# A fused transformer kernel: the last attention output ahead of the gate's exponents, half 1's logits ahead of half 0's score rows, and the eighth expert's second layer in PSUM bank 0

## The chip, the cores and the metric

The program runs on one core of one Trainium2 chip. The metric is the device time of one execution in microseconds (us), the median of three runs. The profile is one further execution of the same program, recorded by the hardware profiler.

## The reference, cut to what matters

The input x has 2 sequences of 512 tokens of width 128, and the context has 2 times 154 rows. Four blocks are added to x in turn, each fed with its layer norm:

```python
x = x + _L0_xattn_ref(_layernorm(x), ctx, ctx, Wq, bq, Wk, bk, Wv, bv, Wo, bo)   # 16 heads of width 8
x = x + _L0_ffn_ref(_layernorm(x), gate_w, ln_w, ln_b, fc1s, b1s, fc2s, b2s)     # 8 experts, each picks 128 of 1024 tokens
x = x + _L1_xattn_ref(_layernorm(x), ctx, mask, W_attn)
x = x + _L1_ffn_ref(_layernorm(x), Wr, br, ...)                                  # 32 experts, top 8 of each token
```

The change touches the end of the first block, and the first expert block (`_L0_ffn_ref`), which is

```python
scores = softmax(xf @ gate_w.T, axis=-1)           # 1024 x 8
vals, idx = top_k(scores.T, 128)                   # each expert its 128 best tokens
h   = gelu(layernorm(xf[idx]) * ln_w + ln_b) @ fc1 + b1)
out = (h @ fc2 + b2) * vals                        # 128 x 128 for each expert
xf  = xf.at[idx].add(out)
```

## The kernel before, in words

Everything is written out by hand in Bass: each engine has its own instruction list, and the engines meet only at semaphores. `wait_ge(Z["name"], n)` holds the engine, and all that is queued behind it, until the counter has reached n; the order of the lists is the order of the work. The tokens are cut into two halves of four 128-row tiles (half 0 and half 1, one per sequence). PSUM has 8 banks of 128 x 512 fp32, named by number as `bank[:, n, ...]`.

**End of the first attention.** The heads are worked off in four combos (0 to 3); combos 0 and 1 belong to half 0, combos 2 and 3 to half 1. A combo's weighted values stand in bank 5 (`attend`, L1360). ScalarE copies them to `osb` (`outputs`, L938), TensorE turns them (`out_turned`; the last combo in two parts, `last_out_turned`, into banks 6 and 2), VectorE divides by the row sums (`normalise`, L514 and L515, into `att`), TensorE turns `att` back (`last_back_turned`), ScalarE adds the bias (`with_bias`, L931, into `attT`), TensorE multiplies by Wo (`project`, L1403), and VectorE adds the result to x (`residual`, L523, into `x1`).

**The gate.** For each half TensorE turns x1 (`gate_turn`), ScalarE copies it (`gate_input`, L948), and TensorE multiplies it by the gate's weights (`logits`, L1420). VectorE applies the layer norm's shift and scale to the logits and subtracts the row maximum (`gate_shift`, L536 to L543), ScalarE takes the exponents (`gate_exp`, L953), VectorE divides by the sum and repeats each score 16 times (`gate_scores`, L550 to L555), TensorE turns these (`score_rows`) and ScalarE copies them into `srep` (`gate_rows`, L957). The 128th best score of every expert is then found in eight rounds: VectorE counts (L646, L649), TensorE adds up the counts (L1590), VectorE sets the next candidate (L659 to L675). Half 0's gate is worked off while half 1's attention ends. In the lists before, ScalarE has half 0's `gate_exp` ahead of the last `outputs`; VectorE has half 0's `gate_shift` ahead of the last two `normalise`; TensorE has `score_rows(0)` ahead of `gate_turn(1)` and `logits(1)`.

**Filler on TensorE.** `early_work(n, to)` (L1253) and `idle_work(n, to)` (L1233) issue n bf16 matmuls of 128 x 512 whose result nobody reads, into a bank that is free.

**The eight experts.** In steps e = 0 to 9, TensorE does `slots_of(e, 0)` (L1666), `first_layer(e)` (L1674), `slots_of(e, 1)`, `scatter(e - 2)` (L1694, L1695) and `second_layer(e - 1)` (L1682, L1684). The second layer always writes bank 4; ScalarE reads it there (`high_out`, L1097, into `ohi`), VectorE after it (`low_out`, L719, into `olo`), and `scatter` needs both. So `second_layer(e)` waits until `olo_ready` has reached e, that is, until the expert before has been read from the bank. After the last scatter ScalarE copies each half (L1117), and TensorE turns it back.

Of the kernel before, what the change touches and what calls it, by code (L numbers as in the profile page):

```python
# [13 lines left out]
P = 128  # L14
D = 128
# [12 lines left out]
COMBOS = 2 * B  # L28
# [5 lines left out]
E0, F0 = 8, 512  # L34
# [65 lines left out]
def build(nc, x_d, ctx2_d, mask_d, watt_d, pack_d, rows_d, gate_d, fc1_d, fc2_d, wout_d, wr_d, rec_d,  # L100
          bd_d, out_d):
    with ExitStack() as ctx:
# [140 lines left out]
        def f32(ap):  # L243
            return ap.bitcast(F32)
# [42 lines left out]
            return bank[:, (3, 4, 7, 7)[g], 0:B * SK]  # L287

        @block.sync  # L290
        def _(sp):
            sp.dma_start(x[:, 0:TB], x_d[:, 0:TB]).then_inc(L["x0"], 16)
            sp.dma_start(watt[:, 0:24 * QW], watt_d[:, 0:24 * QW]).then_inc(L["watt"], 16)
            sp.dma_start(watt[:, 24 * QW:], watt_d[:, 24 * QW:]).then_inc(L["late"], 16)
            sp.dma_start(x[:, TB:], x_d[:, TB:]).then_inc(L["x1"], 16)
            sp.dma_start(gate[:, :], gate_d).then_inc(L["gate"], 16)
            sp.dma_start(fc1[:, :, :], fc1_d).then_inc(L["fc1"], 16)
            sp.dma_start(fc2[:, :, :, :], fc2_d).then_inc(L["fc2"], 16)
            sp.dma_start(mask[:, :, :], mask_d).then_inc(L["mask"], 16)
            sp.dma_start(wout[:, :, :], wout_d).then_inc(L["wout"], 16)  # L300
            sp.dma_start(wr[:, :], wr_d).then_inc(L["wr"], 16)
            sp.dma_start(bd[:, :], bd_d).then_inc(L["bd"], 16)
            sp.wait_ge(Z["cleared"], 1)
            sp.dma_start(rows[0:1, :], rows_d).then_inc(L["rows"], 16)

            for n in range(3):
                sp.dma_start(rec[:, n, :], rec_d[n]).then_inc(Z["rec_ready%d" % n], 16)
            for n in range(3, PAIRS):
                sp.wait_ge(Z["split_ready"], n - 2)
                sp.dma_start(rec[:, n % 3, :], rec_d[n]).then_inc(Z["rec_ready%d" % (n % 3)], 16)  # L310
            for b in range(B):
                sp.wait_ge(Z["out_ready"], b + 1)
                sp.dma_start(out_d[:, b * TB:(b + 1) * TB], out[:, b * TB:(b + 1) * TB]).then_inc(Z["stored"], 16)
            sp.wait_ge(Z["stored"], 16 * B)
# [109 lines left out]
        def _(dve):  # L424
# [19 lines left out]
            def aggregate(n, twice=False):  # L444
                h = (n - 1) % 2
                for i in range(TB):
                    ins = dve.bn_aggr(mv[:, h, i, :], stats[:, h, i, :])
                link(ins)
                dve.tensor_scalar(negmean[:, h], mv[:, h, :, 0], -1.0, None, ALU.mult)
                dve.tensor_scalar_add(vareps[:, h], mv[:, h, :, 1], EPS).then_inc(Z["var_ready"], 1)  # L450
                if twice:

                    dve.tensor_scalar(vtwice[:, h], mv[:, h, :, 1], 1.0 + EPS, EPS * EPS, ALU.mult, ALU.add)\
                        .then_inc(Z["twice_var"], 1)
                return n
# [48 lines left out]
            def normalise(c, part=None):  # L504

                g = c % 2
                dve.wait_ge(Z["aq_psum"], c + 1 + (part or 0))
                if c == 2:
                    dve.wait_ge(Z["at_psum"], 1)
                i0, i1 = (0, TB) if part is None else (2 * part, 2 * part + 2)  # L510
                turned_ = bank[:, 7 if part is None else (6, 2)[part], i0 * P:i1 * P].rearrange("p (n c) -> p n c", c=32)
                to = att[:, i0 * P:i1 * P].rearrange("p (n g h d) -> p n g h d", g=2, h=2, d=DH)[:, :, g]
                n = 4 * (i1 - i0)
                link(dve.reciprocal(rden[:, 4 * i0:4 * i1, :], turned_[:, :, 2 * DH:2 * DH + 2]))  # L514
                dve.tensor_tensor(to, turned_[:, :, 0:2 * DH].rearrange("p n (h d) -> p n h d", h=2),  # L515
                                  rden[:, 4 * i0:4 * i1, :, None].broadcast_to([P, n, 2, DH]), ALU.mult)\
                    .then_inc(Z["att_ready"], 1)
# [28 lines left out]
            def gate_scores(b):  # L546

                ts = slice(b * TB, (b + 1) * TB)
                dve.wait_ge(Z["lgexp_ready"], b + 1)
                link(dve.tensor_reduce(small[:, 1, ts], lg[:, ts], AX.X, ALU.add))  # L550
                link(dve.reciprocal(small[:, 2, ts], small[:, 1, ts]))
                dve.tensor_tensor(sc[:, ts], lg[:, ts], small[:, 2, ts, None].broadcast_to([P, TB, E0]), ALU.mult)\
                    .then_inc(Z["sc_ready"], 1)
                dve.wait_ge(Z["sc_ready"], b + 1)
                dve.tensor_copy(screp[:, ts], sc[:, ts, :, None].broadcast_to([P, TB, E0, P // E0]))\  # L555
                    .then_inc(Z["screp_ready"], 1)
# [66 lines left out]
            dve.wait_ge(Z["x1_ready"], 1)  # L623
            n = measure(x1, 0, twice=True)
            normalise(2)
            dve.wait_ge(Z["gsum_ready"], 1)
            gate_shift(0, n)
            for part in range(2):
                normalise(COMBOS - 1, part)
            gate_scores(0)  # L630
            norms[0] += 1
            n = norms[0]
            for a in range(2):
# [3 lines left out]
                    ins = dve.bn_stats(stats[:, (n - 1) % 2, i, :], x1[:, TB + i, :])  # L637
            link(ins)
            aggregate(n, twice=True)
            gate_shift(1, n)  # L640
            gate_scores(1)

# [73 lines left out]
            def low_out(e):  # L716

                dve.wait_ge(Z["ohi_ready"], e + 1)
                dve.scalar_tensor_tensor(olo[:, e, :], bank[:, 4, 0:D], wslot[:, e:e + 1], f32(ohi[:, e, :]),  # L719
                                         ALU.mult, ALU.subtract).then_inc(Z["olo_ready"], 1)  # L720

            for t in range(T):
# [12 lines left out]
            n = []  # L735
# [154 lines left out]
        def _(act):  # L890
# [150 lines left out]
            exponents(3, 8)  # L1041
            exponents(3, 9)
            gate_input(0)
            gate_exp(0)
            for c0, c1 in ((0, S // 2), (S // 2, S)):
                outputs(COMBOS - 1, c0, c1)
            for c0, c1 in ((0, S // 2), (S // 2, S)):
                with_bias(1, c0, c1)
            gate_rows(0)
            gate_input(1)  # L1050
            gate_exp(1)
            gate_rows(1)
            for b in range(B):
# [39 lines left out]
            def high_out(e):  # L1093

                act.wait_ge(Z["fc2_psum"], e + 1)
                act.wait_ge(Z["w_ready"], 1 + 2 * e // E0)
                act.activation(ohi[:, e, :], bank[:, 4, 0:D], ACT.Copy, scale=wslot[:, e:e + 1])\  # L1097
                    .then_inc(Z["ohi_ready"], 1)

            gathered(0)  # L1100
# [124 lines left out]
        def _(pe):  # L1225
            def turn(dst, src, n=P):
                return pe.transpose(dst, src, ident[0:n, 0:n])  # L1227
# [150 lines left out]
            def last_out_turned(part):  # L1378
                if part == 0:
                    take6(Z["att_ready"], COMBOS)  # L1380
                else:
                    pe.wait_ge(Z["lgsub_ready"], 1)
                pe.wait_ge(Z["osb_ready"], COMBOS + part)
                for i in (2 * part, 2 * part + 1):
                    ins = turn(bank[:, 2 if part else 6, i * P:(i + 1) * P], osb[:, i * P:(i + 1) * P])
                ins.then_inc(Z["aq_psum"], 1)

            def last_back_turned(part):
# [173 lines left out]
            pe.wait_ge(Z["consts_ready"], 6)  # L1562
            for part in range(2):
                last_out_turned(part)
            for part in range(2):
                last_back_turned(part)
            project(1)
            score_rows(0)
            gate_turn(1)
            idle_work(3, 5)  # L1570
            logits(1)
            idle_work(9, 5)
            score_rows(1)

            pe.wait_ge(L["wout"], 16)
# [101 lines left out]

            def second_layer(e):
                pe.wait_ge(Z["hid_ready"], FT * (e + 1))
                if e:  # L1680
                    pe.wait_ge(Z["olo_ready"], e)
                pe.matmul(bank[:, 4, 0:D], onesrow[:, :], rows[:, e * D:(e + 1) * D], start=True, stop=False)  # L1682
                for f in range(FT):
                    ins = pe.matmul(bank[:, 4, 0:D], hid[:, e % 2, f, :], fc2[:, e, f, :], start=False,  # L1684
                                    stop=(f == FT - 1))
                ins.then_inc(Z["fc2_psum"], 1)

# [12 lines left out]
            for e in range(E0 + 2):  # L1700
                if e < E0:
                    slots_of(e, 0)
                    first_layer(e)
                    slots_of(e, 1)
                if e >= 2:
                    scatter(e - 2)
                if e == 0:
                    gather_scores(0)
                if e in (1, E0 // 2):
                    slot_scores(2 * e // E0)  # L1710
                if 1 <= e <= E0:
                    second_layer(e - 1)
                gather(1, *SECOND_PICKS.get(e - 1, (0, 0)))
                if e == E0 // 2 - 1:
                    gather_scores(1)
# [272 lines left out]
```

## Time and profile before

| | us |
|---|---|
| median of 3 runs | 264.9 |
| lowest and highest run | 264.27, 265.03 |
| profiled execution, its own time | 263.52 |
| profiled execution, span from first to last instruction | 261.7 |
| TensorE busy | 232.6 (89%) |
| VectorE busy | 185.6 (71%) |
| ScalarE busy | 133.6 (51%) |
| GpSimd busy | 65.8 (25%) |
| mean granted TensorE clock | 0.986 of full speed |

Times in views of the trace are counted from the span's start. The chain of waits is followed back from the last instruction: each row is a piece of work that the end waited for. A row "x8" merges eight instructions of a line.
### The profile page before, as it was taken

What the parts mean: (1) busy time and instruction counts of PE and PEld (TensorE: products, weight loads), DVE (VectorE), ACT (ScalarE), POOL (GpSimd) and SP (SyncE); (2) the same over time, 40 slices, a digit from 0 to 9 for tenths busy, and PEclk for the clock granted to TensorE, in tenths of its full rate; (3) what the DMA queues carried; (4) which work ended last, traced back from release to release, by engine and by line L of the source; (5) the groups of instructions that cost most, each with busy time, mean ns of one, the idle gap of its engine ahead of it and who ended that gap; (6) DMA issues with size and microseconds to landing.
All of it is one profiled execution on the core that took longest, in us unless ns stands there. A gap on an engine that the chain in (4) does not pass through costs nothing.

```text
span 261.7 us, 3695 instructions
## 1 busy us (share of the span) xinstructions
PE 232.6 (89%) x1222; PEld 162.6 (62%) x1232; DVE 185.6 (71%) x452; ACT 133.6 (51%) x271; POOL 65.8 (25%) x104
## 2 busy tenths in 40 slices
PE   8989999999685659899998869796999999999993
PEld 3547454744552226587787558584788888888871
DVE  2798976924557878583253475899988888888883
ACT  2458487777229601532442436756654445555451
POOL 6335800203061200000670030210053443535000
PEclk9999999999889997999999999999999999999999
DMA  6991000000000000000150000000012113110002
GB/s 234 412 387 68 0 0 1 3 0 3 0 0 0 0 1 3 0 3 0 34 149 24 0 0 3 1 0 0 0 43 56 65 44 82 40 40 0 3 0 80
DMA packets 5140, 11.61 MB, mean 44 GB/s; under 512 B 801, under 2 KB 1921, under 8 KB 4866
## 3 DMA queue, kind: packets, MB, share of 16 engines
q1 hardware_dynamic: 4290, 10.61, 12.0%
q10 hardware_dynamic: 832, 0.78, 0.9%
q8 instruction: 10, 0.16, 0.3%
q14 instruction: 8, 0.07, 0.1%
HBM read 10.86 MB, written 0.52 MB: 43 GB/s over the span
## 4 chain that ended last, share of the span: by engine, by line
PE 73%; DVE 17%; ACT 4%; issue 3%; POOL 1%; DVEq 0%; ACTq 0%; POOLq 0%
PE bank L1227 5%; PE bank L1799 5%; PE bank L1803 5%; PE bank L1800 5%; PE bank L1360 5%; PE bank L1346 4%; DVE att L646 4%; PE bank L1301 4%; PE bank L1833 3%; PE bank L1836 3%; PE bank L1834 3%; PE bank L1684 3%; PE bank L1674 3%; PE bank L1283 3%; PE bank L1814 3%
## 5 line engine op out<-in xcount | busy, mean ns | idle before, releaser
L1166 ACT ACTIVATE arena_d<-bank,bias 128x512 f32<-128x512 f32 x34 | 23.4, 689 | 31.8 <-PE bank L1803 31.8
L822 DVE SCALAR_TENSOR_TENSOR arena_d<-bank,bias,arena_d 128x512 f32<-128x512 f32 x34 | 25.5, 750 | 9.5 <-ACT arena_d L1166 9.3
L502 DVE TENSOR_REDUCE smax<-bank 128x3 f32<-128x462 f32 (+2 forms) x44 | 25.4, 620 | 5.9 <-PE bank L1301 5.6
L1799 PE MATMUL bank<-arena_b 128*128 128x512 f32 x68 | 26.7, 393 | 0.1
L1803 PE MATMUL bank<-arena_b 128*128 128x512 f32 x68 | 26.5, 390 | 0.0
L1800 PE MATMUL bank<-arena_b 128*128 128x512 f32 x68 | 26.5, 390 | 0.0
L973 ACT ACTIVATE arena_c<-bank 128x512 f32<-128x512 f32 x40 | 22.6, 598 | 7.1 <-PE bank L1346 3.3
L408 POOL CAST arena_b<-rec 128x512 fp32r<-128x512 f32 x17 | 13.4, 790 | 46.6 <-PE bank L1836 46.5
L836 DVE TENSOR_TENSOR arena_a<-arena_d,arena_a 128x512 fp32r<-128x512 f32 x34 | 23.5, 690 | 0.8 <-ACT arena_a L1173 0.7
L708 DVE TENSOR_SCALAR arena_a<-bank,pack 128x512 fp32r<-128x512 f32 x16 | 12.0, 751 | 15.7 <-PE bank L1666 13.1
L1173 ACT CAST arena_a<-arena_d 128x512 fp32r<-128x512 f32 x34 | 20.8, 613 | 3.4 <-DVE arena_d L831 3.1
L831 DVE TENSOR_TENSOR arena_d<-arena_d,bank 128x512 f32<-128x512 f32 x32 | 21.8, 681 | 0.4 <-PE bank L1814 0.3
L326 POOL TENSOR_TENSOR rstd<-vareps,neghalf 128x4 f32<-128x4 f32 x8 | 8.1, 1014 | 51.9 <-DVE vareps L450 51.9
L1233 PE MATMUL bank<-pack,onesb 128*128 128x512 bf16 x70 | 18.5, 395 | 0.5 <-issue 0.2
L1301 PE MATMUL bank<-arena_a 96*128 96x462 f32 (+3 forms) x64 | 17.7, 358 | 0.4 <-DVE smax L502 0.3
L1346 PE MATMUL bank<-arena_a 100*128 100x512 f32 x40 | 17.7, 468 | 0.0
L411 POOL TENSOR_TENSOR arena_b<-rec,arena_b 128x384 fp32r<-128x384 f32 x17 | 16.4, 963 | 1.4
L1301 PEld LDWEIGHTS bank<-arena_a 96*128 96x128 f32 x64 | 11.3, 189 | 8.2 <-issue 3.7
L1836 PE MATMUL bank<-arena_a,arena_b 128*128 128x512 f32 x34 | 13.7, 402 | 1.2 <-DVE arena_a L836 1.0
L1799 PEld LDWEIGHTS bank<-arena_b 128*128 128x128 f32 x68 | 12.8, 188 | 3.1 <-issue 0.3
L1800 PEld LDWEIGHTS bank<-arena_b 128*128 128x128 f32 x68 | 12.8, 188 | 2.7
L1803 PEld LDWEIGHTS bank<-arena_b 128*128 128x128 f32 x68 | 12.8, 188 | 2.7
(246 smaller groups left out, 493.8 us busy)
## 6 DMA issues: line engine op xcount, KB each, us to landing
rec<-in_rec SPq DMA_DIRECT2D x17, 257.0 KB, 2.6
arena_d<-in_fc SPq DMA_DIRECT2D x1, 2048.0 KB, 10.7
fc<-in_fc SPq DMA_DIRECT2D x1, 2048.0 KB, 15.0
x<-in_x SPq DMA_DIRECT2D x2, 256.0 KB, 4.3
out<-x SPq DMA_DIRECT2D x2, 256.0 KB, 2.0
watt<-in_watt SPq DMA_DIRECT2D x1, 384.0 KB, 4.4
pack<-in_pack ACTq DMA_DIRECT2D x1, 382.0 KB, 5.4
ctx<-in_ctx ACTq DMA_DIRECT2D x2, 154.0 KB, 7.3
```

Of the source, the lines that this page charges most:

```text
L502: dve.tensor_reduce(dst, src, AX.X, ALU.max).then_inc(Z["max_done"], 1)
L822: dve.scalar_tensor_tensor(to[:, k % 2, :], bank[:, 2 + k % 2, :], bias[:, u % SPLITS, 1:2], sil[:, k % 2, :], ALU.add, ALU.mult).then_inc ...
L831: dve.tensor_tensor(hh[:, k % 2, :], gu[:, k % 2, :], bank[:, 5 - k % 2, :], ALU.mult)\
L836: dve.tensor_tensor(hlo[:, k % 2, :], hh[:, k % 2, :], f32(hhi[:, k % 2, :]), ALU.subtract)\
L973: act.activation(pT[:, n % RING, :], bank[:, 3 + n % 2, :], ACT.Exp, scale=float(DH) ** -0.5)\
L1166: act.activation(sil[:, k % 2, :], bank[:, k % 2, :], f, bias=bias[:, STEPS[k][0] % SPLITS, 0:1])\
L1301: return pe.matmul(to, qs[0:3 * QW, cc % QSLOTS, t * P:(t + 1) * P], ks[0:3 * QW, cc, k0:k1], start=True, stop=True)
L1346: pe.matmul(bank[:, 3 + n % 2, :], ks[0:KQ, cc, j * P:(j + 1) * P], qs[0:KQ, cc % QSLOTS, :], start=True, stop=True).then_inc(Z["score_psu ...
L1799: pe.matmul(d, whi[:, r, w], y3hi[:, cs], start=True, stop=False)
L1800: pe.matmul(d, wlo[:, r, w], y3hi[:, cs], start=False, stop=False)
L1803: ins = pe.matmul(d, whi[:, r, w], y3lo[:, cs], start=False, stop=True)
L1836: pe.matmul(d, whi[:, r, w], hlo[:, k % 2, :], start=False, stop=(k == LAST[b]), skip_group_check=True)\
```

## The change

ScalarE's list has half 0's `gate_exp` behind the last `outputs` and `with_bias`, and `gate_rows(0)` behind `gate_input(1)`. VectorE's list has the last two `normalise` ahead of half 0's `gate_shift`, and `gate_scores(0)` behind the residual and the statistics of half 1. TensorE's list has `logits(1)` ahead of `score_rows(0)`, the second turned part goes to bank 3 in place of bank 2 and no longer waits for `lgsub_ready`, and ten more filler matmuls are spread over the stretch (2, 2, 3 and 3), while the 3 and 9 of before become 6. In the expert stage, the eighth expert's second layer writes bank 0, doesn't wait for the seventh expert's `olo`, and stands ahead of the seventh expert's scatter.

```diff
+        def second_bank(e):
+            return 4 if e < E0 - 1 else 0
@@ VectorE
-                turned_ = bank[:, 7 if part is None else (6, 2)[part], i0 * P:i1 * P].rearrange("p (n c) -> p n c", c=32)
+                turned_ = bank[:, 7 if part is None else (6, 3)[part], i0 * P:i1 * P].rearrange("p (n c) -> p n c", c=32)
@@
             normalise(2)
+            dve.wait_ge(Z["att_ready"], COMBOS - 1)
+            for part in range(2):
+                normalise(COMBOS - 1, part)
             dve.wait_ge(Z["gsum_ready"], 1)
             gate_shift(0, n)
-            for part in range(2):
-                normalise(COMBOS - 1, part)
-            gate_scores(0)
...
             aggregate(n, twice=True)
+            gate_scores(0)
             gate_shift(1, n)
             gate_scores(1)
@@ low_out on VectorE, and likewise high_out on ScalarE
-                dve.scalar_tensor_tensor(olo[:, e, :], bank[:, 4, 0:D], wslot[:, e:e + 1], f32(ohi[:, e, :]),
+                dve.scalar_tensor_tensor(olo[:, e, :], bank[:, second_bank(e), 0:D], wslot[:, e:e + 1], f32(ohi[:, e, :]),
@@ ScalarE
             gate_input(0)
-            gate_exp(0)
             for c0, c1 in ((0, S // 2), (S // 2, S)):
                 outputs(COMBOS - 1, c0, c1)
             for c0, c1 in ((0, S // 2), (S // 2, S)):
                 with_bias(1, c0, c1)
+            gate_exp(0)
+            gate_input(1)
             gate_rows(0)
-            gate_input(1)
             gate_exp(1)
             gate_rows(1)
@@ TensorE
             def last_out_turned(part):
                 if part == 0:
                     take6(Z["att_ready"], COMBOS)
-                else:
-                    pe.wait_ge(Z["lgsub_ready"], 1)
                 pe.wait_ge(Z["osb_ready"], COMBOS + part)
                 for i in (2 * part, 2 * part + 1):
-                    ins = turn(bank[:, 2 if part else 6, i * P:(i + 1) * P], osb[:, i * P:(i + 1) * P])
+                    ins = turn(bank[:, 3 if part else 6, i * P:(i + 1) * P], osb[:, i * P:(i + 1) * P])
@@
                 last_out_turned(part)
+            pe.wait_ge(Z["att_ready"], COMBOS - 1)
+            early_work(2, 7)
             for part in range(2):
                 last_back_turned(part)
+            early_work(2, 7)
             project(1)
+            early_work(3, 5)
+            gate_turn(1)
+            early_work(3, 5)
+            logits(1)
             score_rows(0)
-            gate_turn(1)
-            idle_work(3, 5)
-            logits(1)
-            idle_work(9, 5)
+            idle_work(6, 5)
             score_rows(1)
@@
             def second_layer(e):
                 pe.wait_ge(Z["hid_ready"], FT * (e + 1))
-                if e:
+                if 0 < e < E0 - 1:
                     pe.wait_ge(Z["olo_ready"], e)
-                pe.matmul(bank[:, 4, 0:D], onesrow[:, :], rows[:, e * D:(e + 1) * D], start=True, stop=False)
+                to = bank[:, second_bank(e), 0:D]
+                pe.matmul(to, onesrow[:, :], rows[:, e * D:(e + 1) * D], start=True, stop=False)
...
+                if e == E0:
+                    second_layer(E0 - 1)
                 if e >= 2:
                     scatter(e - 2)
...
-                if 1 <= e <= E0:
+                if 1 <= e < E0:
                     second_layer(e - 1)
```

## Rows read from the trace of the kernel before

**Rows 1.** The page: the chain that ended last, by engine.
```profile
PE 73%; DVE 17%; ACT 4%; issue 3%; POOL 1%; DVEq 0%; ACTq 0%; POOLq 0%
```

**Rows 2.** Chain of waits, 65 to 80 us: start us, us, what.
```profile
65.24 1.00 PE bank L1420 x8
...
67.37 0.36 ACT osb L938
...
67.87 0.42 PE bank L1227 x2
...
68.61 0.30 DVE att L515
...
69.43 0.48 ACT attT L931
...
70.05 1.92 PE bank L1403 x8
71.96 1.71 PE bank L1227 x8
...
74.44 1.04 PE bank L1420 x8
...
75.57 0.20 DVE lg L539
...
79.44 1.30 DVE att L646 x2
```

**Rows 3.** Windows: us, busy us of PE, PEld, DVE, ACT, POOL, PEclk, DMA, GB/s.
```profile
66.24:70.00 3.76, 1.56 (x8) 0.81 (x8) 2.28 (x12) 1.32 (x5) 0.00 (x0) 1.00 0.00 0
70.20:73.60 3.40, 3.40 (x16) 3.34 (x18) 2.50 (x14) 0.78 (x2) 0.00 (x0) 0.50 0.00 0
94.00:97.40 3.40, 1.41 (x7) 0.42 (x4) 2.58 (x12) 0.00 (x0) 0.00 (x0) 1.00 0.00 0
97.60:100.80 3.20, 2.98 (x30) 1.80 (x31) 1.90 (x6) 0.21 (x1) 0.00 (x0) 0.50 0.02 5
```

**Rows 4.** Chain of waits, 140 to 147 us: the last two experts.
```profile
140.99 0.91 PE bank L1684 x8
...
142.73 0.50 PE bank L1694
...
143.92 0.22 PE bank L1682 x2
...
145.47 0.36 DVE arena_e L719
...
145.88 0.50 PE bank L1694
...
146.65 0.59 ACT xnT L1117
```

**Rows 5.** Chain of waits elsewhere: a projection and filler, at either clock.
```profile
10.61 0.88 PE bank L1253 x4
...
58.65 0.89 PE bank L1403 x8
...
98.94 2.22 PE bank L1233 x5
```

**Rows 6.** Timeline of VectorE, 69 to 74 us: start us, us, instruction.
```profile
69.10 0.29 DVE L515 TENSOR_TENSOR att<-bank,rden 128x128 f32<-128x128 f32 x1
...
69.95 0.43 DVE L555 COPY arena_c<-sc 128x512 f32<-128x512 f32 x1
71.15 0.42 DVE L523 TENSOR_TENSOR x<-bank,x 128x256 f32<-128x256 f32 x1 [0.77 <-PE bank L1403]
...
72.98 0.38 DVE L447 BATCH_NORM_AGGREGATE mv<-stats 128x2 f32<-128x6 f32 x4
```

**Rows 7.** Timeline, 91 to 105 us: a round's filler on TensorE, VectorE's picks.
```profile
91.41 1.24 PE L1233 MATMUL bank<-pack,onesb 128*128 128x512 bf16 x5
99.80 4.91 DVE L698 TENSOR_TENSOR arena_b<-pack,slot 128x512 fp32r<-128x512 f32 x8
```

More of the change, by code:

```diff
@@ L1096, in high_out @@
                 act.wait_ge(Z["w_ready"], 1 + 2 * e // E0)
-                act.activation(ohi[:, e, :], bank[:, 4, 0:D], ACT.Copy, scale=wslot[:, e:e + 1])\
+                act.activation(ohi[:, e, :], bank[:, second_bank(e), 0:D], ACT.Copy, scale=wslot[:, e:e + 1])\
                     .then_inc(Z["ohi_ready"], 1)
@@ L1679, in second_layer @@
                 pe.wait_ge(Z["hid_ready"], FT * (e + 1))
-                if e:
+                if 0 < e < E0 - 1:
                     pe.wait_ge(Z["olo_ready"], e)
-                pe.matmul(bank[:, 4, 0:D], onesrow[:, :], rows[:, e * D:(e + 1) * D], start=True, stop=False)
+                to = bank[:, second_bank(e), 0:D]
+                pe.matmul(to, onesrow[:, :], rows[:, e * D:(e + 1) * D], start=True, stop=False)
                 for f in range(FT):
-                    ins = pe.matmul(bank[:, 4, 0:D], hid[:, e % 2, f, :], fc2[:, e, f, :], start=False,
+                    ins = pe.matmul(to, hid[:, e % 2, f, :], fc2[:, e, f, :], start=False,
                                     stop=(f == FT - 1))
```

## The prediction

> **What bounds the kernel now.** I read the page first, for the chain that ended last by engine: 73% of it is TensorE and 17% VectorE [rows 1]. So the kernel is a serial walk with TensorE full in most stages, and what counts is the few stretches in which the chain hops between engines. The chain in order of time shows two, and the change sits in both.
>
> The first is from the last attend to the first count of the score search, 65.24 to 79.44 us [rows 2]. The reader is to see how small its pieces are. TensorE does half 0's logits until 66.24. Then nothing runs on it until 67.87, although the last combo's weighted values had been in PSUM since 65.24. ScalarE copied them only at 67.37, because `gate_exp(0)` is ahead of that copy in its list and waits for four VectorE steps on the logits. From 67.87 on the work is a strict relay: turn, divide, turn back, bias, project.
>
> Next I read the windows, for the clock. TensorE was busy 1.56 us of 3.76 between 66.24 and 70.00, all of it turns but for the first bit of a projection at the end, and from 70.2 to 73.6 it ran at the granted clock 0.50, the lower level of 1.2 GHz [rows 3]. In that stretch stand the projection and half 1's turns, 1.92 and 1.71 us [rows 2]; the same projection at the upper level, 2.4 GHz, took 0.89 [rows 5]. The same happened at 97.6 after a stretch in which TensorE was busy 1.41 of 3.40 us [rows 3].
>
> The second is the end of the expert stage, 140 to 147 us [rows 4]. The second layer of expert 6 (counted from 0) ends at 141.90. ScalarE and VectorE then read it, TensorE scatters it from 142.73, does the second layer of expert 7 until 145.05, and waits again, for the same two readers, until 145.88. TensorE's hole is paid twice with nothing beside it.
>
> **Edit 1, the order of the last attention output and the gate.** I rebuild the stretch from 65.24. All durations are of this one profiled execution; where a step runs at the upper clock afterwards, I take the row that has it there.
>
> ScalarE is free (its copy of half 0's input ended earlier), so it copies `osb` from 65.27 on, in two pieces, until about 65.9. That lies beside the logits, so the turns start when those end: 66.27 in place of 67.87, 1.60 earlier. The second turned part has no wait for `lgsub_ready` any more, and bank 3 is free by then, the exponents of the score block in it having been taken before the attend. Turns to last `att` took 67.87 to 69.39 [rows 2, 6]; the same 1.5 gives 67.8, with the first `att` at 67.3 (68.90 before).
>
> TensorE after its turns (0.88 for both parts, four turned tiles) is at 67.15. The new wait for `att_ready` 3 is met since 62.8 and costs nothing. Two fillers at 0.22 each [rows 5] take it to 67.6, 0.3 past the first `att`: this is a cost, since the turning back could have started at 67.35. Back turns end at 68.03 and 68.47, the bias of the first part is there at 68.53 (0.48, rows 2), and two more fillers hold TensorE until 68.9. So the fillers cost about 0.35 of the relay's gain in all, and the projection starts at 68.93 in place of 70.05.
>
> The projection now follows a dense stretch, and I take it at the upper clock, 0.89 [rows 5]. Its first half is there after 0.5, so the residual starts at 69.43 against 71.15 [rows 6]: 1.72 earlier. VectorE then runs from piece to piece as before; `aggregate` starts at 71.26 in place of 72.98 [rows 6]. VectorE's own order has to be looked at: `gate_shift(0)` now follows the normalising, five steps of 0.2 each, 67.8 to 68.9, and is done before the residual. `gate_scores(0)` moves from 69.3 to 70.4, where it was hidden, to behind `aggregate`: three steps of 0.22 and L555 at 0.43 [rows 6], from 71.9 to 73.0, and one more step of half 1's shift to 73.2.
>
> What hides it is TensorE: after the projection at 69.8 come three fillers (70.5), half 1's turns, which need the second residual (70.7) and end at 71.4, ScalarE's copy until 72.0, beside it three fillers until 72.03, and the logits. These took 1.13 from their start to L539 (74.44 to 75.57, rows 2), so 72.03 gives 73.16, and VectorE is free at 73.2. The two meet within 0.05; if the cover were gone, each 0.1 us of TensorE's that is saved would be worth nothing. L539 starts at 73.2 against 75.57: 2.35 earlier.
>
> Behind it, `score_rows(0)` takes 0.44 on TensorE beside VectorE's steps, and `gate_rows(0)` (0.59) now stands ahead of `gate_exp(1)` on ScalarE, until about 74.2, where the subtraction is done at 74.1: 0.07 late. The rest is as before. The filler of 6 in place of 9 ends at 74.9, before half 1's score rows at 75.8; GpSimd's fills still lie beside L555. The first count starts at 77.15 in place of 79.44. **Edit 1 is worth 2.3 us.** Its parts were 1.6 from ScalarE's order, less 0.5 to the projection (fillers, and the readers), plus the clock.
>
> Here a rule of the Trainium skill speaks against the change. What the row shows is that 1.56 us of nearly nothing but turns in 3.76 did not keep the clock [rows 3]. The page "TensorE: Matmul & The Clock Gate", section "Part 4: PE-mode transpose", says that work in transpose mode does not count as activity as matmuls do. The trace agrees as far as it goes. The new order has turns in the same place; by that rule only the fillers and the projection hold the clock. What it would cost is the first rival.
>
> **Edit 2, the eighth expert's second layer.** After 141.90 TensorE goes straight on with the second layer of expert 7: its hidden values were ready at 140.5, bank 0's last reader is long past, and the wait for `olo` is gone. It takes 0.22 + 0.91 [rows 4] and ends at 143.03. Expert 6 is read meanwhile, which took 0.83 from the layer's end to the scatter (141.90 to 142.73, rows 4), so it is waiting. Its scatter follows at once, four matmuls of 0.23, 0.27 less than the 1.19 of before (142.73 to 143.92) since it follows without a gap: 143.96. Expert 7 is read in that time, until 143.03 + 0.78 = 143.81 (145.05 to 145.83 before), so the last scatter starts at 143.96 against 145.88: 1.92, and its first pair, again without a start from idle, 0.48 against 0.75: up to 0.27 more. ScalarE's copy, 146.65 before [rows 4], comes at about 144.5. Bounds 1.9 and 2.2; **I take 2.1.** The margin between reader and scatter is 0.15, so the stretch is bounded by TensorE afterwards. What follows is a relay on the critical chain (turn, residual, statistics), which passes the gain on whole.
>
> **The sum.** 2.3 + 2.1 = 4.4. The profiled execution took 263.5 (span 261.7), which gives 259.1. The runs' median is 264.9, 1.4 above it; I take off the same 4.4 and get **260.5**.
>
> **Rivals.** (a) The clock falls in the first stretch all the same. The turns between 66.3 and 68.5 are like those of before; for it speaks that row, against it that four fillers and the projection add 1.8 us of matmuls to 66.3 to 69.8 and close the holes. Fallen from 70.2 to 73.6, the remaining fillers take 0.44 each (2.22 for 5, rows 5), half 1's turns 1.71 [rows 2]: fillers until 70.8, turns until 72.5, ScalarE 73.1, fillers until 73.75, logits to 74.9 against 73.2. That is 1.7 lost: 262.2.
>
> (b) The clock falls elsewhere, because the work shifts by 2.3 and 4.4 us. In the search a round has 1.24 us of filler in some 2.1 to 2.3 us [rows 7]; at the lower clock five fillers take 2.2 and TensorE becomes later than VectorE by 0.3 a round, or 0.5 in all. The relay after the experts could lose up to 1.5. I price it at 1.0: 261.5.
>
> (c) The fall at 97.6 vanishes. It slows the fillers ahead of the slots' turns [rows 5]; without it the turns come about 1.3 earlier, but VectorE's picks, 4.91 from 99.8 [rows 7], then bound the gather, and 0.9 is left: 259.6.
>
> (d) Slower than before. It needs one thing, the lower clock from 70 on that does not end: 1.7 as in (a), 0.3 in each of seven rounds, 2.1, and then 0.21 for each of sixteen gathering matmuls. It decides if it lasts past about 101 us; until 105 it costs 7, 267.5. Against it: both low stretches of before ended within 3.4 us with TensorE full [rows 3].
>
> (e) Edit 2 brings nothing, because the readers or the banks hold the last scatter where it was: 262.6. Against it, the times of the rows leave 0.15 of room and the last scatter can slip by 1.9 before it comes to this.
>
> **How the numbers follow.** Forecast 0.60 (its own range 259.2 to 261.3), (a) 0.14, (b) 0.11, (c) 0.08, (d) 0.03, (e) 0.04. A measurement of this kernel can tell about 0.3%, 0.8 us, from no change. All but (d) are over 0.8 below 264.9, and I leave 0.03 for (a) and (e) together or worse: faster 0.94, same 0.03, slower 0.03. The range takes in (a), (b), (c) and the unexplained 1.4 between the profile and the median: 258.7 to 262.4.
>
> **What would show it.** In the profile after: `osb` L938 at 65.3, ahead of the gate's exponents; turns from 66.3; the projection at about 68.9 for 0.9 us; granted clock 1.00 from 70 to 74; the first count near 77.2. With 2.3 us taken off all later times, TensorE without a hole between expert 6's second layer and the last scatter, and the copy L1117 4.4 to 4.5 earlier than before. The sum is wrong if the clock is 0.50 in the first stretch, if L539 waits for VectorE's `gate_scores(0)` by more than 0.1, or if ScalarE's `gate_rows(0)` holds the exponents by more than 0.2.

## The result and the profile after

The kernel after took 261.12 us (median of 4 runs, 260.7 to 261.63), the one before 264.58 (4 runs, 263.32 to 265.03). The ratio is 0.9887 (0.986 to 0.9914). The forecast was 260.5 with a range from 258.7 to 262.4: right in sign and range, 0.6 us too low in time, and too large in the gain, 4.4 us against 3.5 by the medians and 2.5 by the profiled executions (span 261.7 before, 259.2 after). The forecast also put the profiled execution at 259.1; it took 261.02, 1.9 more.

The first stretch of the chain after, to be held against [rows 2] (start us, us, what; helper lines moved by 5: L1227 is now L1232):

```profile
65.54 0.99 PE bank L1423 x8
66.53 0.29 PE bank L1232 x2
...
67.69 0.30 DVE att L519
...
68.48 0.43 PE bank L1258 x2
68.91 0.46 PE bank L1406 x4
...
69.39 0.43 DVE x L527
...
71.92 1.03 PE bank L1423 x8
...
75.08 1.24 DVE arena_c L559
...
77.67 1.30 DVE att L651 x2
```

The "x4" row is only the first half of the projection, which is all that the first residual waits for. The timeline has the whole of it, to be held against the 1.92 of before:

```profile
68.74 1.05 PE L1406 MATMUL bank<-watt,attT 128*128 128x128 f32 x8
```

The turns follow the logits without a gap, the projection runs at the upper clock, and half 1's logits start at 71.92. From the start of half 0's logits (65.17 and 65.47 in the timelines) to the first count it took 14.27 us before and 12.20 after: 2.07 gained. One row doesn't fit the forecast: the copy L559 takes 1.24, where the same copy for half 0 took 0.43.

The second stretch, the last two experts, against [rows 4]:

```profile
139.00 0.89 PE bank L1692 x8
139.89 0.22 PE bank L1690 x2
140.12 0.89 PE bank L1692 x8
141.01 0.24 PE bank L1702
...
141.95 0.40 PE bank L1702
142.35 0.25 PE bank L1703
...
142.62 0.59 ACT xnT L1122
```

TensorE has no hole. From the end of expert 6's second layer to ScalarE's copy it took 4.75 before (141.90 to 146.65) and 2.73 after (139.89 to 142.62): 2.02 gained.

So the copy came 4.03 earlier, and yet the span ended only 2.5 earlier. The windows of the relay behind the experts show why (us, busy us of PE, PEld, DVE, ACT, POOL, PEclk, DMA, GB/s):

```profile
146.40:149.80 3.40, 1.64 (x7) 0.65 (x5) 2.65 (x14) 1.25 (x3) 2.23 (x3) 1.00 0.00 0
149.80:153.20 3.40, 3.14 (x13) 3.12 (x14) 1.54 (x6) 0.21 (x1) 0.00 (x0) 0.51 0.00 0
```

The clock is at its lower level, 1.2 GHz, through half 0's cross scores. The chain of both kernels there, before and then after:

```profile
154.09 1.31 PE bank L1738 x8
155.41 0.44 PE bank L1227 x4
```
```profile
150.06 2.42 PE bank L1748 x8
152.48 0.85 PE bank L1232 x4
```

From the copy to the first context matmul it took 14.19 us before (146.65 to 160.84) and 15.72 after (142.62 to 158.34): 1.53 given back. Everything behind that took 100.86 in both. The sum closes: 2.07 + 2.02 - 1.53, with 0.24 more from the stages between the gate and the last experts, and 0.30 less because half 0's logits started 0.3 later in this execution, is 2.5.

### The profile page after: what moved, and what is told of

The parts are those of the page before. It is cut to its first block, busy times and chain, and to the rows that moved or that the text cites. A ratio compares the mean times of both kernels' runs of the same rounds, so it can differ in the third digit from the quotient of the medians.

```text
span 259.2 us, 3712 instructions
## 1 busy us (share of the span) xinstructions
PE 234.3 (90%) x1236; PEld 162.8 (63%) x1236; DVE 186.2 (72%) x452; ACT 133.3 (51%) x271; POOL 65.7 (25%) x104
## 4 chain that ended last, share of the span: by engine, by line
PE 73%; DVE 18%; ACT 4%; issue 3%; POOL 1%; DVEq 0%; ACTq 0%; POOLq 0%
PE bank L1809 5%; PE bank L1813 5%; PE bank L1810 5%; PE bank L1232 5%; PE bank L1365 5%; PE bank L1351 4%; DVE att L651 4%; PE bank L1306 4%; PE bank L1258 3%; PE bank L1843 3%; PE bank L1846 3%; PE bank L1681 3%; PE bank L1844 3%; PE bank L1692 3%; PE bank L1824 3%
```

## The experiments

Eleven programs were run: ten edits, and the kernel after once more (e11). All stage times below are read from the one profiled execution of each, in the same way, while the median is that of all its runs. "Gate" is from the start of half 0's logits to the first count, "experts" from the end of expert 6's second layer to ScalarE's copy, "relay" from that copy to the first context matmul, "threshold" from the threshold's turn to the first gathering matmul; "low" is where the granted clock was 0.50, to about 0.2 us. Every execution was at the lower level in its last 1 to 3 us too, which the table leaves out. A stage that the table doesn't have lies between "threshold" and "experts": from the first gathering matmul to the end of expert 6's second layer it took 40.06 to 40.11 in eight executions, 40.35 in e2, 40.5 in e3, e5 and e6, and 40.94 in e10.

The medians come from four sets of runs, each with runs of before beside it. The medians of before were 264.58 (first comparison), 264.34 (beside e1 to e4), 263.59 (beside e5 to e8) and 264.56 (beside e9 to e11), so a difference of a few tenths between kernels of different sets says nothing.

| kernel | median | gate | threshold | experts | relay | low, us from the span's start |
|---|---|---|---|---|---|---|
| before | 264.58 | 14.27 | 5.27 | 4.75 | 14.19 | 70.2-73.6, 97.5-100.9 |
| after | 261.12 | 12.20 | 5.02 | 2.73 | 15.72 | 95.3-98.7, 149.9-153.3 |
| e1, expert part alone | 263.18 | 14.91 | 5.36 | 2.73 | 15.80 | 68.0-75.0, 98.6-102.2, 153.2-156.8 |
| e2, gate part alone | 262.78 | 12.20 | 6.27 | 4.75 | 14.20 | 80.8-84.4, 94.6-101.6 |
| e3, without the ten fillers | 261.03 | 12.56 | 5.04 | 2.73 | 14.19 | 73.9-77.3, 97.6-101.2 |
| e4, GpSimd's fills early | 260.46 | 11.41 | 5.38 | 2.73 | 15.81 | 95.4-99.0, 150.0-153.8 |
| e5, filler in the relay | 260.05 | 12.19 | 6.14 | 2.73 | 14.19 | 81.0-84.6, 94.8-101.8 |
| e6, new place, bank 4 | 262.75 | 12.19 | 5.11 | 3.88 | 15.82 | 96.8-100.4, 151.4-155.0 |
| e7, bank 0, old place | 261.68 | 12.20 | 5.23 | 4.75 | 14.19 | 92.2-99.4 |
| e8, exponents first | 261.14 | 12.20 | 5.43 | 2.73 | 15.81 | 96.0-99.6, 150.6-154.2 |
| e9, e4 + e5 + e8 | 259.6 | 11.20 | 5.00 | 2.73 | 14.19 | 80.2-83.8, 93.8-97.4, 165.6-169.2 |
| e10, e9 and filler in the search | 257.95 | 11.20 | 3.81 | 2.73 | 14.19 | none before the last 1 us |
| e11, after once more | 261.1 | 12.20 | 5.44 | 2.73 | 15.80 | 96.2-99.8, 150.8-154.4 |

### e1: the expert part alone

The list of before, with `second_bank(e)` and the shorter wait in `second_layer` as in the change, and these edits:

```diff
+                if e == E0:
+                    second_layer(E0 - 1)
                 if e >= 2:
                     scatter(e - 2)
...
-                if 1 <= e <= E0:
+                if 1 <= e < E0:
```

> The kernel before with only the expert part: the eighth expert's second layer in bank 0, ahead of the seventh's scatter. Theory: the relay between the last two experts loses its second hole. From the end of expert 6's second layer to ScalarE's copy of the scattered half it took 4.75 us before (141.90 to 146.65) and 2.73 after (139.89 to 142.62), so here 2.7, and the search before it stays as it was, 14.2 us from the last attend to the first count. The time is 2.0 below before, 262.6, plus or minus 1.5 for where the low clock falls. Rival (the readers or the banks hold the last scatter, and the gain came from the shift of the earlier part): 4.7 and the time of before.

The experts took 2.73, as the theory had it, so the gain is the edit's own. But the time fell only by 0.8 to 1.2 us (ratio 0.9971, 0.9948 to 0.9994; medians 264.34 and 263.18), and the profiled execution shows what can take the rest: the low level met the relay, 15.80 against 14.19, and lay over the whole gate, which took 14.91 against 14.27:

```profile
68.00:75.00 7.00, 6.36 (x26) 5.07 (x27) 4.41 (x22) 2.19 (x6) 0.29 (x1) 0.51 0.00 0
```

### e2: the gate part alone

The kernel after with `second_bank(e)` returning 4 for all e, and `second_layer` in its old place and with its old wait.

> The kernel after, with the expert part as before: bank 4 throughout and the old place. Theory: from the last attend's end to the first count 12.1 us as after, against 14.2 before; the last two experts take 4.75 as before. Time 262.5, 2.1 below before. Whether the low clock meets the relay behind the experts, which cost 1.5 us in the kernel after, depends on where it falls in this execution. Rival: the low level in that relay is something the gate's new order brings with it, wherever the work stands in time; then it is there here too, and the relay from ScalarE's copy to the first context matmul takes 15.7 us as after, and not 14.2 as before.

The gate took 12.20 and the experts 4.75: the two parts are independent. Ratio 0.9923 (0.9898 to 0.9948). The relay was at 14.20, so the gate's new order does not bring the low level there by itself. The rival falls, and e1, which has the old gate and met it, speaks against it too.

What does bring it is not shown. Of the executions without filler in the relay, six of the seven with the second layer ahead of the scatter met it (after, e1, e4, e6, e8, e11; not e3) and none of the three with the old place did (before, e2, e7). That the new place of the expert's layer favours it is thus a rival that no run settles. The traces show one thing more. In each of these six the fall in the relay begins 54.6 us after the fall near 97, while the work has shifted: ScalarE's copy stands 46.4 to 47.4 us behind that fall where the relay was met, and 45.9, 49.1, 51.4 and 52.8 where it was not. So the fall kept its distance from the earlier fall and not from the work.

The search can lose to the low level as well. Here it lay at 94.6 to 101.6, over the whole threshold stage, and that took 6.27 against 5.02 after. The turns of the slots alone, the second row, took 1.92 against 1.04 after:

```profile
96.83 2.75 PE L1238 MATMUL bank<-pack,onesb 128*128 128x512 bf16 x6
99.37 1.92 PE L1232 MATMUL bank<-pack,slot 128*8 128x128 f32 x8
```

### e3: without the ten fillers

```diff
-            early_work(2, 7)
             for part in range(2):
                 last_back_turned(part)
-            early_work(2, 7)
             project(1)
-            early_work(3, 5)
             gate_turn(1)
-            early_work(3, 5)
             logits(1)
```

> The kernel after without its ten added filler matmuls between the last attend and half 1's logits. Theory (the fillers hold the clock): the granted clock falls to 0.50 somewhere between 67 and 74 us, the projection or half 1's turns take about twice 0.89 us, and although 0.4 us of filler ahead of the projection is gone the first count comes 0.3 to 1.5 us later than after, 12.4 to 13.6 from the last attend; the time is 0.3 to 1.5 above after, 261.4 to 262.6. Rival (turns and the denser order hold the clock by themselves): clock 1.00 throughout, the first count 0.4 earlier, 11.7 from the last attend, and a time 0.4 below after.

The outcome is between the two. The clock did fall, but only behind the projection, the turns and the logits:

```profile
73.90:77.20 3.30, 3.00 (x9) 1.27 (x8) 1.96 (x5) 0.64 (x2) 2.20 (x6) 0.50 0.00 0
```

The gate took 12.56, 0.36 more than after, as half 1's score rows were turned in 0.99 us in place of 0.67. The dense order alone kept the projection and half 1's turns at the upper clock: between 66.2 and 70.2 TensorE was busy 3.08 of 4.00 us, where before it was 1.56 of 3.76. That the missing filler brought the fall at 73.9 rests on this one execution; none of the ten others with the new gate order had a fall between 66 and 80. The median is that of after (261.03 and 261.12), and the profiled execution is 0.5 shorter, since its relay was spared. What I had charged for the fillers was wrong too: without them the projection started 3.23 us after half 0's logits (65.59 to 68.82), with them 3.27 (65.47 to 68.74). In e3's chain TensorE starts 0.14 after the step that it waited for, ahead of L1232 (67.62 to 67.76) and ahead of L1406 (68.69 to 68.82). In after's chain, where filler keeps it busy, the rows of L1258 and L1406 follow each other without such a gap.

### e4: GpSimd's fills early

```diff
                 pool.tensor_tensor(rplus[:, b], ...)
+                if b == 0:
+                    pool.wait_ge(Z["pv_done"], len(ROUNDS) * COMBOS)
+                    pool.memset(slotT[:, :].bitcast(F32), 0.0).then_inc(Z["cleared"], 1)
+                    pool.memset(sm[:, :, :], MASKED).then_inc(Z["sm_filled"], 1)
-            pool.wait_ge(Z["pv_done"], len(ROUNDS) * COMBOS)
...
```

> The kernel after with GpSimd's two fills (slotT and the softmax's padding) ahead of half 1's reciprocal roots, at 65.6 to 67.2 us, in place of 74.4 to 76.0. Theory: the fills slow VectorE's copy of half 1's scores, which took 1.24 us after and 0.43 for half 0 with the same shape; here it takes 0.43 to 0.5 again, and the first count comes 0.75 earlier, 11.4 from the last attend; time 260.4. The price is looked for at VectorE's L518 and L519 at 66.9 to 68, which take 0.3 each with no fill beside them. Rival: the copy is slow for a reason of its own (its clock in the list, the shape's place in SBUF), it stays at 1.24 and nothing moves.

The theory holds: gate 11.41, copy 0.43, median 260.46. The profiled execution is only 0.1 shorter than after's, as its threshold stage took 0.36 more and its logits started 0.18 later. The timelines of after and then of e4 (start us, us, engine, line, instruction):

```profile
74.90 1.12 POOL L389 MEMSET arena_c<- 128x1232 f32 x1
75.08 1.23 DVE L559 COPY arena_c<-sc 128x512 f32<-128x512 f32 x1
```
```profile
66.28 1.13 POOL L390 MEMSET arena_c<- 128x1232 f32 x1
67.09 0.26 DVE L519 RECIPROCAL rden<-bank 128x16 f32<-128x16 f32 x1 [3.79 <-PE bank L1233]
...
75.26 0.43 DVE L560 COPY arena_c<-sc 128x512 f32<-128x512 f32 x1
```

VectorE's reciprocal, which reads PSUM, took 0.26 beside a fill, as without one (L518 at 66.91 in after). The copy reads and writes SBUF. In after it ended 0.29 after the fill's end (74.90 + 1.12 = 76.02, and 76.31), so it wasn't slowed in proportion but held. Not every VectorE step in SBUF is: the three small ones ahead of the copy (L554 to L556, 74.42 to 75.04) ran beside the two fills (74.44 to 76.02) in 0.18 to 0.19 each, as for half 0. The page "SBUF — State Buffer" of the Trainium skill, section "SBUF: two separate sides", says that GpSimd and such a VectorE copy lock a shared pair of ports in turn, whole instructions at a time; the three overlaps seen here (before and e8 follow) agree that the copy is blocked until the fill's end. The timeline of the kernel before has it too:

```profile
76.67 1.12 POOL L385 MEMSET arena_c<- 128x1232 f32 x1
77.42 0.65 DVE L555 COPY arena_c<-sc 128x512 f32<-128x512 f32 x1
```

There the copy met only the fill's last part, took 0.65, and ended 0.28 after it; the change moved the copy 2.3 earlier, and the fills only 1.8.

### e5: filler in the relay

```diff
-            idle_work(12, 5)
+            idle_work(17, 5)
...
             inputs_turned(0)
+            idle_work(2, 5)
             cross_scores(0)
```

> The kernel after with 17 in place of 12 fillers behind the turns that follow the last scatter, and 2 more ahead of half 0's cross scores, both where TensorE waited (147.0 to 148.3 and 149.4 to 150.06 us). Theory: the low level of 149.8 to 153.2 came after a stretch in which TensorE was busy 1.64 of 3.40 us and cost 1.5; with the holes filled the clock stays at 1.00 and from ScalarE's copy L1122 to the first context matmul it takes 14.2 us as before, not 15.7; time 259.7. Rival: turns and filler do not hold it, or the fillers come in the way of the turns: 14.2 to 15.7 and a time as after, 261.1.

The relay took 14.19: the holes are filled, the clock stays up there, and the fillers are in nobody's way. e9 and e10, which have these fillers too, also took 14.19. As some executions without them were spared as well, three executions make the effect likely and don't prove it.

```profile
147.00:150.40 3.40, 3.13 (x15) 1.34 (x13) 3.23 (x20) 0.88 (x2) 1.62 (x3) 1.00 0.00 0
150.40:153.80 3.40, 3.16 (x23) 2.59 (x23) 2.01 (x7) 1.13 (x2) 0.62 (x1) 1.00 0.00 0
```

The median, 260.05, is 1.1 below after's, but the ratio to the runs beside it, 0.9859 (0.9819 to 0.9898), is only 0.003 below after's, and the two intervals overlap. In the profiled execution the low level lay in the search instead (81.0 and 94.8 to 101.8): the threshold took 6.14, 1.1 more than after, and the span is that of after within 0.1.

### e6 and e7: place and bank apart

e6 is after with bank 4 for all experts, and the wait for `olo_ready` back in `second_layer(7)`, which stays ahead of `scatter(6)`. e7 is after with bank 0, and `second_layer(7)` behind `scatter(6)`.

> The kernel after with the eighth expert's second layer in its new place ahead of the scatter, but in bank 4 and so behind the seventh's readers. Theory: the second layer starts 0.83 later, but the last scatter then finds its readers done, so from the end of expert 6's second layer to ScalarE's copy it takes 2.73 + 0.83 = 3.55 us, against 4.75 before and 2.73 after: the order is worth 1.2 and the bank 0.8. Time 0.8 above after, 261.9. Rival (the bank is what counts and the order nothing): 4.7 and 263.1.

> The kernel after with bank 0 for the eighth expert's second layer, but in the old place behind the seventh's scatter. Theory: the scatter ahead of it already waits for what the second layer no longer waits for, so the bank alone changes nothing: 4.75 us from the end of expert 6's second layer to ScalarE's copy, and the time 2.0 above after, 263.1. Rival (bank 4 being read while it is written slowed something): less than 4.5.

The bank alone is worth nothing (experts 4.75), the place alone 0.87 (3.88), both together 2.02. e6's chain:

```profile
140.48 0.36 DVE arena_e L724
...
140.97 0.46 PE bank L1690 x2
141.43 0.89 PE bank L1692 x8
142.32 0.24 PE bank L1702
...
143.93 0.59 ACT xnT L1122
```

I had expected 3.55. The second layer takes 1.35 here and not 1.11, since it starts from idle (0.46 for L1690, 0.22 after), and it starts 0.92 after expert 6's layer ended, not 0.83. e7's time, 261.68, is only 0.6 above after's and not 2.0 (0.9921 against 0.9887 by the ratios, 0.9 us). In its profiled execution the experts take 2.0 more, and the relay isn't met, which gives 1.5 of it back. e6's median, 262.75, is 1.6 above after's, from 10 runs between 260.77 and 263.68. Both show that a shift of the work and the clock can't be told apart by medians.

### e8: half 1's exponents ahead of half 0's row copy

```diff
             gate_input(1)
+            gate_exp(1)
             gate_rows(0)
-            gate_exp(1)
             gate_rows(1)
```

> The kernel after with half 1's exponents ahead of half 0's score rows on ScalarE. Theory: the exponents waited for the copy L962 by about 0.2 us (subtraction done at 73.94, exponents at 74.16), so the first count comes 0.2 earlier, 11.9 us from the last attend, unless GpSimd's fills, which stand still, then cover more of VectorE's copy; time 260.9 to 261.1, which this measurement can't tell from after, so the trace decides. Rival: half 0's row copy now ends later and holds the count: 12.1 or more.

The exponents came 0.2 earlier, but the gate stayed at 12.20, by the condition that the expectation named:

```profile
74.49 1.42 DVE L559 COPY arena_c<-sc 128x512 f32<-128x512 f32 x1
74.51 1.12 POOL L389 MEMSET arena_c<- 128x1232 f32 x1
```

The copy ended at 75.91, 0.28 after the fill. What was gained ahead of it, it waited away. By these rows the copy started 0.02 ahead of this fill and was held all the same; the fill before it ran until 74.58.

### e9, e10 and e11: together, and the search's end

e9 is e4, e5 and e8 together. e10 adds this around the last rounds of the search:

```diff
-                    idle_work(5, 5)
+                    idle_work(8 if k + 2 == len(SHIFTS) else 5, 5)
+            idle_work(1, 5)
             pe.wait_ge(Z["prefix_ready"], len(SHIFTS) - EXACT + 1)
             turn(bank[:, 6, 0:P], prefix...)
+            idle_work(2, 5)
```

> The kernel after with the three edits that were tried alone: GpSimd's fills early, half 1's exponents ahead of half 0's row copy, and the fillers in the relay behind the experts. Theory: the fills hid what the exponents' place was worth, so together they give more than apart: the first count 11.2 us from the last attend (12.2 after, 11.4 with the fills alone, 12.2 with the exponents alone); the relay 14.2. Time 1.6 below after, 259.4. Rival (the exponents' place is worth nothing): 11.4.

> The same with fillers where TensorE waited around the last round of the search: 8 in place of 5 behind the seventh round, 1 behind the eighth, 2 behind the threshold's turn. Theory: the low level that every execution so far had between 92 and 102 us comes from that stretch of 1.4 busy in 3.4; with the holes filled it doesn't come, and from the threshold's turn to the first gathering matmul it takes 4.3 in place of 5.0 to 6.3 us; time 0.9 below e9, 258.6. Rival (b): the fillers stand ahead of the turn and of the small matmuls, each costs 0.1 to 0.2, and VectorE's picks bound the gather anyway: same time as e9 or 0.3 more.

> The kernel after once more, unchanged, as the measure for the other two of this call on the same chip. The theories expect 261.1 and a first count 12.2 us from the last attend. The relay behind the experts is expected at 15.7 us where the low clock meets it and at 14.2 where it does not: the same program should show either, if the place of the low level is set by when it falls and not by the program.

e9: the gate took 11.20, so the exponents' place is worth 0.2 once the fills are gone. The median is 259.6, 1.5 below e11's 261.1.

e10: 257.95 us, ratio to before 0.9766 (0.9736 to 0.9796), 3.15 below after. It beats both kernels. The chain shows the fillers at the upper clock, 1.29 for six, where after has 2.19:

```profile
95.56 1.29 PE bank L1239 x6
96.86 0.92 PE bank L1233 x8
97.78 0.24 PE bank L1645
```
```profile
96.98 2.19 PE bank L1238 x6
99.17 0.87 PE bank L1232 x8
100.05 0.24 PE bank L1642
```

The threshold took 3.81, better than the 4.3 expected. But most of that is given back at once. VectorE's picks (L704), which the gathering matmuls need, take 4.91 us for eight in both kernels, and start 3.27 us behind the threshold's turn in e9 and 2.91 in e10, only 0.36 earlier. So TensorE gathers at their pace now: a pair of matmuls each 0.60 us in e10's chain, where e9's takes 0.46:

```profile
98.72 0.37 PE bank L1645
99.09 0.23 PE bank L1646
99.31 0.38 PE bank L1645
99.69 0.23 PE bank L1646
```

From the first gathering matmul to the end of expert 6's second layer it took 40.94 against e9's 40.10. The threshold and this stage together are 0.35 shorter than e9's (44.75 against 45.10), so rival (b) was right about the gather. The profiled execution is 1.2 shorter than e9's mainly for another reason. e9 met the lower level once more behind the relay, at 165.6, and everything from the first context matmul on took 102.0 there and 100.9 in e10. In e9's chain a matmul of that stage takes 0.43 us until 169, and 0.23 behind it:

```profile
166.28 0.43 PE bank L1811
...
169.69 0.23 PE bank L1811
```

e10 has no more filler there than e9. Why the fall at 165.6 didn't come is open.

The mean granted clock of the six runs is 0.989 to 0.999, and the runs lie within 0.42 us (257.86 to 258.28), where e11's lie within 1.47 (260.53 to 262.0) and the ten runs of before beside it within 1.82.

e11: the relay met the low level again, as in after, and took 15.80. Its expectation was that the same program should show either value; the two traces of it both show the higher one. Its six runs have mean clocks from 0.975 to 0.985, so they meet more or less of the lower level, but only one of them has a trace. Where the low stretches lie in the others stays open.

## Why the prediction was right, point by point

**Edit 1 as a whole, 2.3.** It measured 2.07, but by two errors that cancel in part. From the start of half 0's logits to L539 (L543 after) I had 8.03 us (65.17 to 73.2) and it took 7.59 (65.47 to 73.06), 0.44 better. From there to the first count I had 3.95 and it took 4.61, 0.66 worse. The next points say where most of it lies.

**ScalarE's order, the turns at 66.27.** Right: the turns started 0.99 us behind the start of half 0's logits (65.54 to 66.53), where the forecast had 1.03 (65.24 to 66.27).

**The fillers' price, 0.35.** Wrong: e3 shows 0.04, since they take the place of a start from idle.

**The projection at the upper clock, rival (a).** Right, and rival (a) did not come. Its ground, the rule that turns don't hold the clock, is not settled: e3 kept the upper level through the same stretch with turns, the projection and no filler. The runs don't refute the rule, because the projection's matmuls are in it. No run has the turns alone in so dense an order.

**`gate_scores(0)` and the logits meet within 0.05.** Right: the copy of `gate_scores(0)` ended at 72.93 and the logits at 72.95. L543 started at 73.06, 0.1 after the logits as before. **`gate_rows(0)` 0.07 late**: it was 0.2 (e9 against e4), since the exponents were wanted at 73.95 already, and `score_rows(0)` took 0.67 where I had 0.44.

**"GpSimd's fills still lie beside L555."** This is the step of edit 1 that was mis-sized. I saw the overlap and priced it at the 0.65 of before. But the fills follow the reciprocal roots (1.8 earlier, from vareps at 71.9) and the copy moved by 2.3, so it met nearly the whole of the longer fill: 1.23, 0.58 more. e4 takes it out.

**Edit 2, 2.1.** Right: 2.02, in every kernel that has both the new place and bank 0.

**Rival (b), the clock falls elsewhere.** It came true in the profiled execution, beside the gains of the forecast and not in their place. I gave it 0.11 and 1.0 us; it was in the relay, and cost 1.53. The profile before had the warning: TensorE was idle for 1.36 us ahead of L1227 at 152.38 there. In the rounds of the search, where I named 0.5, a low stretch cost about 0.1 (e2: 17.22 us from first count to threshold, 17.11 after). Behind the rounds it can cost over 1 us, which I didn't price: the threshold took 6.27 in e2 and 6.14 in e5.

**Rival (c), no fall at 97.** It did not come by the shift, 95.3 in place of 97.5. e10 has no low level there, with filler, and what is left of it behind the picks is 0.35 and not my 0.9. **Rivals (d) and (e)** did not come.

**The 1.4 between profile and median, left unexplained.** The fourth run of before took 263.32. Of the ten runs beside e10, four took 263.26 to 263.40 at a mean clock of 0.987 to 0.993, and six 264.46 to 265.08 at 0.969 to 0.980: the runs of before fall into two groups about 1 us apart, and the profiled one (263.52) was of the better kind. The mean clock alone doesn't sort them. Beside e5 to e8, five runs of before took 263.48 to 263.62 at a clock of 0.979, as in the upper group, so it matters where the low level lies and not only how long it lasts. This also says how far the time of the forecast was luck: it was 1.9 off for the profiled execution and 0.6 off for the median. The median of before had about 1.1 to 1.4 in it that its profile didn't, the kernel after's had 0.1, and the gain, taken off the profile, had not allowed for the 1.53 in the relay. The two cancel in large part.

## What to carry to other kernels

Where a kernel's stages are relays, a change that moves work in time also moves it against whatever slows a fixed stretch: price every neighbour that doesn't move with it, here GpSimd's fills (0.58 us) and the stretch in which TensorE goes to its lower clock (1.5 us). Try filler in TensorE's waits of each relay: here it cost 0.04 us in front of a step (e3), and the kernel with all of it (e10) was both the fastest and the steadiest. Look behind the stage that you shorten: e10 took 1.2 us off the threshold and kept 0.35 of it. When a step moves in one engine's list, look at what its new neighbour on each other engine holds, since a gain ahead of a held instruction is worth nothing until the holder is moved (e8 against e9).

## What the runs showed of the hardware

A fill on GpSimd held VectorE's 128x512 fp32 copy from SBUF to SBUF until it ended: in before, after and e8 the copy ended 0.28, 0.29 and 0.28 us after the fill's end, and took 0.65, 1.23 and 1.42 us, by where it started; without the fill 0.43. A reciprocal that reads PSUM beside a fill took 0.26, as alone, and so did small VectorE steps in SBUF (0.18 to 0.19). The second layer's bias matmul, two instructions, took 0.22 us behind other matmuls and 0.46 behind a wait (e6). In six executions of five kernels two falls of TensorE's granted clock, near 97 us and in the relay, began 54.6 us apart, wherever the work stood.
